# Row 0 of x loaded in two halves of H, its second half turned between the first products, 8 filling transposes in place of 13

## The reference, cut to what matters

```python
def _gemma_mlp(x, gate_w, up_w, down_w):
    g = jnp.einsum('bsh,hi->bsi', x, gate_w)
    u = jnp.einsum('bsh,hi->bsi', x, up_w)
    return jnp.einsum('bsi,ih->bsh', jax.nn.gelu(g, approximate=True) * u, down_w)

# layer 0: each row b has two experts, chosen and weighted by its logits
out = sum over the chosen experts e of  w[b, e] * _gemma_mlp(x, skill_gate[e], skill_up[e], skill_down[e])
out = out + _gemma_mlp(x, shared_gate, shared_up, shared_down)
x = x + out
# layer 1
x = x + (x @ W_base.T + b_base + 2.0 * (LoRA of x, with the row's logits as weights))
```

## Time and profile before

| what | value |
|---|---|
| median of 3 runs | 797.0 us (796.98 to 797.44) |
| the profiled execution | 796.85 us |
| its span in the profile | 795.0 us |
| PE busy | 789.5 us, 99% of the span, 4133 matmuls |
| PEld / DVE / ACT / POOL busy | 681.1 / 668.8 / 478.5 / 278.4 us |
| DMA | 105.21 MB, mean 132 GB/s |
| HBM read / written | 79.86 MB / 24.64 MB |

### The profile page before, as it was taken

One profiled execution on the slowest core, in us unless ns is written; L12 is line 12 of the kernel. 1 busy time (PEld: TensorE's weight loads), 2 busy tenths in 40 slices (PEclk: granted clock), 3 DMA queues, 4 the chain that ended last, 5 costly groups with the idle time before them and its releaser, 6 DMA issues.

```text
span 795.0 us, 13413 instructions
## 1 busy us (share of the span) xinstructions
PE 789.5 (99%) x4133; PEld 681.1 (86%) x4133; DVE 668.8 (84%) x910; ACT 478.5 (60%) x737; POOL 278.4 (35%) x284
## 2 busy tenths in 40 slices
PE   8999999999999999999999999999999999999998
PEld 7888888888888888888888889888898888898887
DVE  4866888888887899889888898888898889889886
ACT  6554564564664666656666666666666666566653
POOL 1621321321430363263352444425435234532520
PEclk9999999999999999999999999999999999999999
DMA  7436506304726632563563275346336426631400
GB/s 204 123 80 200 144 1 198 121 1 146 233 72 206 222 116 80 171 184 101 165 189 95 90 224 153 105 141 189 106 125 215 124 80 198 172 108 51 133 2 27
DMA packets 138894, 105.21 MB, mean 132 GB/s; under 512 B 62928, under 2 KB 131280, under 8 KB 138832
## 3 DMA queue, kind: packets, MB, share of 16 engines
q1 hardware_dynamic: 138832, 104.53, 43.7%
HBM read 79.86 MB, written 24.64 MB: 131 GB/s over the span
## 4 chain that ended last, share of the span: by engine, by line
PE 99%; DMA 0%; DVE 0%; ACT 0%; SPq 0%; DVEq 0%; issue 0%
PE ps_ring L827 61%; PE ps_acc L827 36%; DMA raw<-_L_cond_shared_gate_dram 0%; PE ps_acc L1039 0%; PE ps_ring L848 0%; PE ps_ring L853 0%; PE ps_ring L857 0%; PE ps_acc L1059 0%; DVE stage L1925 0%; PE ps_acc L944 0%; PE ps_ring L1059 0%; ACT xc L1165 0%; PE ps_acc L1085 0%; ACT wide L1165 0%; SPq L517 0%
## 5 line engine op out<-in xcount | busy, mean ns | idle before, releaser
L827 PE MATMUL ps_ring<-xc,wide 128*128 128x512 f32 (+1 forms) x1926 | 416.2, 364 | 0.0
L827 PEld LDWEIGHTS ps_ring<-xc,wide 128*128 128x128 f32 x1926 | 336.8, 189 | 59.4 <-DVE post L1568 0.6
L1165 ACT CAST inner_hi<-post 128x512 fp32r<-128x512 f32 x192 | 117.7, 621 | 102.9 <-DVE post L1857 31.8
L827 PE MATMUL ps_acc<-inner_hi,wide 128*128 128x512 f32 x504 | 171.0, 390 | 0.0
L1511 DVE TENSOR_TENSOR inner_lo<-post,inner_hi 128x512 fp32r<-128x512 f32 x192 | 146.3, 769 | 9.0 <-ACT inner_hi L1165 6.1
L1168 ACT ACTIVATE post<-ps_ring 128x512 f32<-128x512 f32 (+1 forms) x125 | 68.0, 546 | 103.4 <-PE ps_ring L827 98.0
L827 PEld LDWEIGHTS ps_acc<-inner_hi,wide 128*128 128x128 f32 x504 | 94.8, 188 | 19.1
L827 PE MATMUL ps_acc<-inner_lo,wide 128*128 128x512 f32 x252 | 98.4, 391 | 0.0
L1168 ACT ACTIVATE post<-post 128x256 f32<-128x256 f32 (+1 forms) x98 | 53.7, 563 | 53.4 <-DVE post L1798 36.3
L827 PE MATMUL ps_acc<-inner_hi,sh_dn 128*128 128x512 f32 x256 | 83.9, 389 | 0.0
L1857 DVE SCALAR_TENSOR_TENSOR post<-post,coef_now,ps_ring 128x512 f32<-128x512 f32 x66 | 49.3, 747 | 36.2 <-PE ps_ring L827 34.1
(11 more groups left out here) (126 smaller groups left out, 1015.5 us busy)
## 6 DMA issues: line engine op xcount, KB each, us to landing
rights_scratch<-xc SPq DMA_DIRECT2D x6, 1792.0 KB, 10.2
raw<-n_L_cond_skill_gate_dram SPq DMA_DIRECT2D x32, 256.0 KB, 3.0
raw<-in_L_cond_skill_up_dram SPq DMA_DIRECT2D x32, 256.0 KB, 3.5
raw<-n_L_cond_skill_down_dram SPq DMA_DIRECT2D x32, 256.0 KB, 3.9
xbuf<-n_L_cond_skill_gate_dram SPq DMA_DIRECT2D x32, 256.0 KB, 3.0
xbuf<-in_L_cond_skill_up_dram SPq DMA_DIRECT2D x32, 256.0 KB, 3.5
xbuf<-n_L_cond_skill_down_dram SPq DMA_DIRECT2D x32, 256.0 KB, 3.8
xt_scratch<-xbuf SPq DMA_DIRECT2D x8, 512.0 KB, 3.3
```

What stands on the lines that cost most here:

```text
L827: last = pe.matmul(dst, left_[a], right_[b], start=start and n == 0, stop=stop and n == len(PASSES) - 1, skip_group_check=adds)
L1165: return nc.scalar.copy(dst, src)
```

## The change

Row 0 of x is loaded by two DMAs of 256 KB, one for each chunk of H, in place of one of 512 KB. The first goes ahead of the gate weights of chunk 0, the second between these and the gate weights of chunk 1. The first raises a new semaphore `x_first`, the second `x_landed[0]`. In DRAM a token's 256 numbers lie together; a half takes 128 of them, so each descriptor run is 512 bytes where it was 4 KB for a partition.

```diff
-            sp.dma_start(x_nat, x_rows[0]).then_inc(x_landed[0], 16)
             for c in range(HC):
+                sp.dma_start(x_nat[:, :, c * P:(c + 1) * P], x_rows[0][:, :, c * P:(c + 1) * P])\
+                    .then_inc([x_first, x_landed[0]][c], 16)
                 sp.dma_start(raw_part(0, GATE)[:, c, :], sg[:, c, 0:PW]).then_inc(gate0_landed[c], 16)
...
                                   start=c == 0, stop=False)
+                    if r == 0 and c == 0:
+                        pe.wait_ge(x_landed[0], 16)
+                        turn(acc[0][1], x_nat, 1)
                     if r == 0:
                         pe.wait_ge(left_ready, c + 1)
...
-            for _ in range(13):
+            for _ in range(8):
                 pe.transpose(ring[3][:, 0:P], ident[:], ident[:])
-            pe.wait_ge(x_landed[0], 16)
-            for c in range(HC):
-                turn(acc[0][c], x_nat, c)
+            pe.wait_ge(x_first, 16)
+            turn(acc[0][0], x_nat, 0)
```

More of the change, by code:

```diff
@@ L277, in cond_resid_kernel @@
         raw_landed = [sem(f"raw_landed{j}") for j in range(PAIRS)]
+        x_first = sem("x_first")
         x_landed = [sem(f"x_landed{r}") for r in range(2)]
```

## The result

The changed kernel takes 799.38 us (799.05 to 800.28, 8 runs), the kernel before 796.94 (796.87 to 797.44, 8 runs): 2.4 us slower, ratio 1.0031, 95% interval 1.002 to 1.0042. The prediction said 797.1, range 796.3 to 798.6, and 8% for rival (b), a TensorE that stays slow long into the products, at 799.7. That rival is what happened.

A forecast was written before the change was run, and what follows sets the result against it. PE was taken to bound the kernel at 99%. An earlier first product (0.46 us) is eaten by moved transposes (0.45); DVE's chain adds +0.05 to a 795.0 span, giving 797.1 us, range 796.3 to 798.6.

The forecast's parts named there:

- rival (b): First products: TensorE's clock stays low until about 11 us, 5.4 us at half speed, +2.7, 799.7 us; 8%.
- a shift ahead of the first up product: PE's stream near the start: any shift there reaches the end in full, up or down.
- The move of four transposes: Between lines 848 and 853: four transposes leave dead time and stand in PE's path, 4 x 0.11 = 0.45 us.
- their removal delays nothing: Filling transposes ahead of x: eight in place of 13 end before the first half lands, so no time changes.
- rival (a): First products: TensorE stays slow into them, from 5.6 to 8.0 us, +1.1, 798.1 us; 22%.
- The gain at the first product: Line 848: starts at 5.62 us (5.42 to 6.22) in place of 6.08, 0.46 gained.
- +0.05: Line 827's first matmul: DVE's chain uses up 0.65 us of slack, start at 8.9 to 9.0, +0.05 us booked.
- The first half of x: First load of row 0: lands at 3.6 us, between an early end of 3.4 and a late one of 4.2.
- dear end: Start loads, late case: 512-byte runs cost 49 ns each, issue 0.25 longer; first half at 4.2, gate weights at 4.97.
- The first gate weights: Gate load of chunk 0: lands at 4.2 us in place of 4.97, with 0.26 MB less in front.
- the second half: Second load of row 0: lands near 5.0 us at no cost, or at worst 6.4, holding the stream 0.3 us.
- the landing at 3.4: First half of x, early end: bytes through at 2.6 us, landed at 3.4, if 512-byte runs go at full rate.

The follow-up runs named there:

- moved turn with a bridge: Kernel before, second four transposes moved behind the first two products, six filling transposes added behind the first four: 797.95 us against 796.94 to 797.19 for the kernel before.
- moved turn: Kernel before with one load of x and 13 filling transposes, the second chunk's four transposes moved behind the first two products: 797.65 us against 796.97.
- changed kernel with 13 fillings: Changed kernel with 13 filling transposes ahead of x in place of its 8: 799.09 us, against 796.97 for the kernel before.
- 8 fillings: Kernel before with 8 filling transposes in place of 13, nothing else changed: 797.74 us against 796.97.
- the three bridges with SP's loads: Filling transposes added behind the first four: 8 in the changed kernel (13 ahead: 798.58 us; 8 ahead: 798.01), 6 in the kernel before with four transposes moved (797.95).
- 8 and a bridge of 8: Changed kernel with its own 8 filling transposes, and 8 more behind the first four transposes of x: 798.01 us, against 796.96 for the kernel before.
- halves by tokens: Kernel before, row 0 of x in two loads of whole tokens (2 KB runs), all eight transposes waiting for both: 799.02 us against 796.96.
- 13 fillings and the bridge of 8: Changed kernel with 13 filling transposes, and 8 more behind the first four transposes of x: 798.58 us, against 796.97 for the kernel before.
- gate weights first: Kernel before with chunk 0's gate weights loaded ahead of undivided row 0 of x, 15 filling transposes in place of 13: 797.99 us against 797.19.
- the runs on ACT's queue: Both gate loads issued by ACT: in the kernel before 801.09 us; in the changed kernel with 13 filling transposes and 8 behind the first four 801.77; against 796.96.

## Why the prediction was wrong, step by step

**Right.** What bounds the kernel, and that a shift ahead of the first up product passes in full: 3.02 us there, 3.02 in the profiled times. That nothing behind it moves. The move of four transposes: priced at 0.45 in the stream, 0.44 in the chain of the moved turn with a bridge, at the fast clock:

```profile
7.13 0.44 PE ps_acc L946 x4
```

The lower heap of the moved turn is 0.6 above the kernel before.

**The failed step** is that of the fillings and the clock: "their removal delays nothing", and in rival (a) "one stop of 0.6 us at 5.5 did not bring the clock down again". The rows behind that sentence show a stop after the rise. The changed kernel has its stops before it. That a clock once up survives 0.6 us says nothing on whether one still low comes up across breaks of 0.5 and 1.0 us. The runs show in its place: with both stops, all 8 runs at 799.05 or more, and 2.6 of the profiled 3.0 us as slow work up to 11.5; with the long one alone, 5 of 11 in the upper heap (moved turn) and 7 of 11 (changed kernel with 13 fillings); with the short one and none before the products, 5 of 11 (8 fillings); with the long one filled, none of 33 stands in a heap apart (the three bridges with SP's loads). A bridge adds transposes as well as closing the break, but the number of fillings alone doesn't sort the kernels: 13 with the break give upper heaps, 8 and a bridge of 8 none. I had the right rival, the right size (799.7 for 799.87 profiled, 799.38 in the median) and gave it 8%, because I held a row about keeping the clock against it.

**Mis-sized.** The gain at the first product, 0.46 by the text, was 0.03; the move of the transposes thus stands uncovered, and by the split above line 829 would have been about 0.4 late at a fast clock, where +0.05 was booked; that alone would have stayed within the range. The first half of x lands at 3.94 and not 3.6: its issue takes 0.72 us and not 0.39 (the dear end had allowed 0.25 more, 0.33 came), and bytes flow only after 2 us. The first gate weights land at 4.99 and not at 4.2, in spite of 0.26 MB less ahead of them, since they were issued at 1.50, not 1.17, and fewer bytes were through: with halves 0.39 MB at 4 us, where 0.69 were before, with the engines idle for two thirds of the time. My dear end took short runs for dear packets (49 ns each); they cost 30 (20 us over 672), and the loss lies in issue time, a later first byte and idle engines. In another run the gate weights land at 4.3 (changed kernel with 13 fillings), and the second half, which I had at 5.0 or at worst 6.4, at 7.3: the landing differs from run to run more than I allowed. For the gate weights the dear end, no gain, is what came.

**The Trainium skill.** The sentence of "TensorE: Matmul & The Clock Gate" (What's actually happening) that the throttled state is the default and sustained activity lifts it fits the changed kernel, whose activity had two gaps and whose clock rose only at 11.5: I should have given it more weight. By itself it doesn't tell the runs apart, for with halves by tokens the clock was up at 5.3 behind a gap of 0.75. Its other sentence, that transposes do not bring the fast clock (PE-mode transpose), is contradicted again: with 13 fillings and the bridge of 8, PE did transposes and nothing else until 6.37, and its first pair of products took 0.70 in place of 1.19. The 512 bytes as smallest run for full rate ("DMA: Bandwidth & Descriptors", Specifications) hold for the engines while they work, 20 GB/s each against 21; the landing at 3.4 that I drew from them does not hold, it was 3.94.

**Left open.** Why the same program falls in one heap or the other, and what in a break decides. Even unbroken work doesn't fix the moment of the rise: it came at 4.6 in the profiled run of the kernel before, past 6 with the moved turn's bridge, and at about 7 with the gate weights first (one short pause), in all three with PE at work from 1.5 on. How much of the late second half is the short runs and how much SP's queue: halves by tokens suggests that both count, the runs on ACT's queue did not separate them. No tried version beats the kernel before.

## What to carry to other kernels

Work that fills dead time on TensorE ahead of the first real product isn't dead: price its removal by the clock, not by the time it seems to hide. Fill every break until the clock is up, above all the one right in front of the products; here a stop of 0.6 us after the rise did no harm, and it proved nothing on one before it. A first load cut into short runs paid here in issue time and delayed what followed it. And look at heaps of runs before believing a median.

## What the runs showed of the hardware that was not expected

- The column of the granted clock reads 1.00 from 6 to 11 us of the changed kernel, while a pair of products takes 0.85 us and later 0.46. At the start of the program only the lengths tell the clock.

```profile
9.00:10.00 1.00, 1.00 (x3) 0.74 (x3) 1.00 (x2) 0.72 (x2) 0.00 (x0) 1.00 1.03 338
```

- A stop of about 0.8 us, 6 us into an 800 us program, goes with heaps of runs 1.9 us apart (moved turn, 797.43 to 797.65 and 799.13 to 799.63); six transposes in it, and there is one heap (797.76 to 798.35).
- PE at work from 1.5 us on without a break, on the same transposes, was fast from 4.6 in one run and still slow past 6 in another.
- A load of 512 runs of 512 bytes holds SP's queue 0.57 to 0.72 us, one of 128 runs of 4 KB 0.39; and the 128 KB load behind it 0.59 us, not 0.42.
- With the gate weights issued from ACT's queue at the same time, row 0 landed at 5.4 in place of 4.1, and the program took 799.3 to 801.5 in all five runs.
